# Small attentions: query, key and value projections from three products of rounded parts, and the context laid out by columns in memory

## The chip, the cores and the metric

One core of one Trainium2 chip runs the kernel. The time is device microseconds (us) of one execution. The engines are TensorE (PE; its weight loads are PEld), VectorE (DVE), ScalarE (ACT), GpSimd (POOL) and SyncE (SP), which here only issues DMAs. SBUF is the on-chip memory, PSUM the eight banks that PE writes.

## The reference

Four transformer layers, one after another, on x (32 sequences of 64 tokens, 256 wide) with a context of the same shape:

```python
x = L0(x, ctx)   # layernorm, self attention; layernorm, cross attention; layernorm, MLP (16 heads of 16)
x = L1(x, ctx)   # a recurrence over the tokens with gates, and a feed-forward part; takes states from ctx
x = L2(x, ctx, ctx)  # two cross attentions with 16 heads of 128, and an MLP
x = L3(x, ctx)   # cross attention with 16 heads of 16, and an MLP
# a small attention (L0 self, L0 cross, L3):
q = (h @ wq + bq); k = (s @ wk + bk); v = (s @ wv + bv)   # s is h or ctx; 256 x 256 weights
out = x + softmax(q @ k.T / 4, masked) @ v @ wo + bo
```

Everything is f32.

## The kernel before, in words

The 2048 tokens go in four chunks of 512 (eight sequences each). Ten stages of four chunks follow one another: self attention, cross attention, MLP, the recurrence and its feed-forward part, two large cross attentions, MLP, the third small attention, MLP. A chunk of a stage has the number `it`; a chunk of a small attention also has `ai`: 0 to 3 self, 4 to 7 cross, 8 to 11 the third. Every engine has its own program, written out by hand as generators that `run` (L364) strings together; engines meet by semaphores only, so that the order written for an engine is the order in which it works.

In a small attention one `n` is four heads of one chunk; p = n % 4 counts them within the chunk. The PE program `attention` (L460) does for each n: `scores` (L490, 32 small products of kbd and qT into banks 0 and 1), `turn` for n - 3 (L509, eight transposes of T into banks 2 and 3) and at the end `weigh` for n - 3 (L519, 32 products of vbd and PTs). Beside them stand, by p: 0, `gather` of ai - 2 and the projections 2 and 3 of ai; 1, `merge` of ai - 2 (the output projection) and `front` (the transposes of the normalised xn for the next chunk); 2, for ai below 4 `ctx_front` (the transposes of one chunk of the context), and `values` of ai + 1; 3, the projections 0 and 1 of ai + 1. Projections (`project` by `linear`, L444) and `values` (L480) are plain f32 products.

All but scores and turn take a bank from a ring of four (banks 4 to 7) in the order in which they are issued: `take` (L389) waits until the one that had the bank four takes earlier has been read by its user. In the third attention's first chunk the ring has two banks.

The other engines follow in the same order of n. DVE (L1419 on): `scale` (scores times mask into T), at p = 3 `values` (adds the bias and writes vbd, in two halves with `largest` between them), `largest` (nmax, of n - 1), `weighed` (reciprocal and a_tok, of n - 4; its end is the semaphore att_out), at p = 1 `update` (X), at p = 3 `stats`. POOL: `masked` (T plus the mask's second part), at p = 0 `roots` (ends with nmr), `lowered` (T minus the largest, of n - 1), at p = 1 `bias` (X<-X,rows). ACT: `exp` of n - 2, `turn` of n - 3 (PTs), at p = 0 `gather`, `project` and `normed` (xn), at p = 1 `front` (hT), at p = 2 the context's copy to ctxT, at p = 3 `project`.

The MLPs and the large attentions already make their products from rounded parts: a number is split into hi (rounded to the type fp32r) and lo = number - hi, and a product is hi hi + hi lo + lo hi, three products of fp32r (`SPLIT`).

## Time and profile before

| | |
|---|---|
| median of 3 runs | 2008.86 us (2006.38 to 2009.13) |
| the profiled execution | 2009.09 us |
| its span in the trace | 2007.3 us |
| PE busy | 95% |
| DVE, ACT, POOL busy | 58%, 52%, 51% |
| mean granted clock of TensorE | 0.973 |

The small attentions take the first 260 us or so and the stretch from 1770 to 1900 us. The span is what the rows below are counted in; matmuls overlap, so the duration of a row with xN is from its first start to its last end, and a mean of one is longer than the distance between two.

### The profile page before, as it was taken

The numbers are of one execution on the slowest core, as the hardware profiler recorded it, in microseconds if no ns is written. First come the engines' busy times: TensorE is split into PE (matmuls) and PEld (weight loads), VectorE is DVE, ScalarE is ACT, GpSimd is POOL, SyncE is SP. The second block draws the span as 40 slices with busy tenths as digits, with TensorE's granted clock in tenths as the row PEclk, the third lists the DMA queues.
The fourth block names the chain that finished last, engine by engine and source line by source line (L and its number), as shares of the span: only waits on it lengthen the run. The fifth ranks groups of instructions, "written<-read, shape, count | busy, mean of one in ns | idle before, by whom it ended". The sixth has DMA issues, their size and how long they took to land.

```text
span 2007.3 us, 39375 instructions
## 1 busy us (share of the span) xinstructions
PE 1901.9 (95%) x15120; PEld 1560.6 (78%) x15120; DVE 1161.2 (58%) x2104; ACT 1046.0 (52%) x1950; POOL 1013.7 (51%) x1140
## 2 busy tenths in 40 slices
PE   8999999898987699999999999999999998999999
PEld 5777789433455488898999989899998988977788
DVE  4556655489888455455545555455455546754654
ACT  4665543433342366665665655566566564445532
POOL 6776831376653255454454545445454454347630
PEclk9999999989997799999999999999999999999999
DMA  5010010000000032332323233233232320000000
GB/s 190 2 44 1 2 56 1 1 0 0 1 1 32 23 107 82 93 88 85 86 88 92 80 93 92 80 93 87 86 89 84 93 69 22 22 24 20 2 11 32
DMA packets 61847, 108.11 MB, mean 54 GB/s; under 512 B 7008, under 2 KB 42336, under 8 KB 60256
## 3 DMA queue, kind: packets, MB, share of 16 engines
q1 hardware_dynamic: 60784, 103.38, 17.0%
q8 instruction: 123, 2.02, 0.4%
q10 hardware_dynamic: 880, 2.22, 0.3%
q14 instruction: 60, 0.49, 0.1%
HBM read 103.47 MB, written 2.10 MB: 53 GB/s over the span
## 4 chain that ended last, share of the span: by engine, by line
PE 82%; DVE 9%; issue 4%; POOL 3%; ACT 2%; DMA 0%; DVEq 0%; SPq 0%; ACTq 0%; POOLq 0%
PE banks L837 19%; PE banks L866 9%; PE banks L909 9%; PE banks L611 7%; PE banks L628 6%; PE banks L447 6%; PE banks L898 6%; PE banks L879 4%; PE banks L456 3%; PE banks L529 2%; PE banks L504 2%; PE banks L486 2%; PE banks L515 2%; PE banks L433 1%; PE banks L887 1%
## 5 line engine op out<-in xcount | busy, mean ns | idle before, releaser
L1882 POOL TENSOR_TENSOR w_lo<-w2ring,w_hi 128x512 fp32r<-128x512 f32 x128 | 166.3, 1299 | 294.7 <-ACT w_hi L1098 294.7
L1322 ACT ACTIVATE PT<-banks 64x256 f32<-64x256 f32 x256 | 96.7, 378 | 262.3 <-PE banks L887 259.2
L1714 DVE SCALAR_TENSOR_TENSOR c_lo<-banks,cols,c_hi 128x512 fp32r<-128x512 f32 x128 | 96.1, 751 | 228.1 <-ACT c_hi L1288 228.1
L1962 POOL TENSOR_TENSOR wo_lo<-wo_ring,wo_hi 128x256 fp32r<-128x256 f32 x128 | 94.0, 735 | 169.1 <-ACT wo_hi L1294 169.1
L909 PE MATMUL banks<-wo_hi,c_hi 128*128 128x256 f32 x512 | 149.9, 293 | 2.7 <-POOL wo_lo L1962 2.7
L909 PE MATMUL banks<-wo_hi,c_lo 128*128 128x256 f32 x512 | 145.1, 283 | 0.0
L909 PE MATMUL banks<-wo_lo,c_hi 128*128 128x256 f32 x512 | 144.8, 283 | 0.0
L898 PEld LDWEIGHTS banks<-PT,v 128*128 128x128 f32 x1024 | 132.7, 191 | 8.9 <-ACT PT L1322 0.4
L898 PE MATMUL banks<-PT,v 128*128 128x128 f32 x1024 | 134.9, 275 | 0.3 <-ACT PT L1322 0.3
L1281 ACT ACTIVATE k<-banks,cols 128x512 f32<-128x512 f32 x128 | 87.9, 687 | 82.8 <-PE banks L837 82.7
L447 PE MATMUL banks<-xm,wl 128*128 128x512 f32 x208 | 109.2, 671 | 16.5 <-DVE xm L1643 6.3
L1723 DVE TENSOR_REDUCE nmax<-banks 128x4 f32<-128x260 f32 x128 | 54.4, 425 | 112.3 <-PE banks L879 112.2
L1920 POOL TENSOR_TENSOR rsZ<-stS,r1T 128x512 f32<-128x512 f32 x64 | 84.7, 1329 | 62.0 <-DVE stS L1591 56.9
L1707 DVE TENSOR_TENSOR v<-banks,dbv 128x512 f32<-128x512 f32 x128 | 88.5, 692 | 46.1 <-PE banks L866 41.6
L1886 POOL TENSOR_TENSOR wv_lo<-w2ring,wv_hi 128x256 fp32r<-128x256 f32 x128 | 113.6, 888 | 0.0
L866 PE MATMUL banks<-wv_hi,ctx_hi 128*128 128x256 f32 x512 | 108.2, 293 | 0.0
L1809 POOL TENSOR_TENSOR T<-T,a_pair 128x1024 f32<-128x1024 f32 x32 | 75.6, 2363 | 63.2 <-DVE T L1443 63.2
L1080 ACT ACTIVATE g_full_a<-banks,cols 128x512 f32<-128x512 f32 x64 | 44.1, 689 | 115.1 <-PE banks L628 113.2
L866 PE MATMUL banks<-wv_hi,ctx_lo 128*128 128x256 f32 x512 | 103.1, 283 | 0.0
L866 PE MATMUL banks<-wv_lo,ctx_hi 128*128 128x256 f32 x512 | 103.1, 283 | 0.0
L967 ACT ACTIVATE xn<-X,nmr,rstd 128x256 f32<-128x256 f32 x160 | 82.8, 591 | 35.5 <-POOL nmr L1777 35.5
L909 PEld LDWEIGHTS banks<-wo_hi,c_hi 128*128 128x128 f32 x512 | 98.2, 192 | 3.1 <-POOL wo_lo L1962 3.1
(224 smaller groups left out, 5599.7 us busy)
## 6 DMA issues: line engine op xcount, KB each, us to landing
w2ring<-in_w SPq DMA_DIRECT2D x128, 384.0 KB, 3.0
b2ring<-in_b SPq DMA_DIRECT2D x128, 128.0 KB, 3.5
wo_ring<-in_wo SPq DMA_DIRECT2D x128, 128.0 KB, 2.3
mlp_w<-in_mlp SPq DMA_DIRECT2D x6, 1024.0 KB, 5.0
wl<-in_wres SPq DMA_DIRECT2D x1, 2688.0 KB, 9.2
X<-in_x_in SPq DMA_DIRECT2D x4, 512.0 KB, 11.4
ctx_tok<-in_ctx_in SPq DMA_DIRECT2D x4, 512.0 KB, 16.9
wb<-in_wres SPq DMA_DIRECT2D x2, 1024.0 KB, 13.0
```

The source lines that it names most:

```text
L447: last = mm(b[0:rows_out, :], w[:, k, m0:m0 + rows_out], src[:, k, :], start=(k == 0), stop=(k == KT - 1))
L611: last = mm(bank[sums(c) + t // 2][:, t % 2 * D:(t % 2 + 1) * D], g[x][:, n % GR, t * P:(t + 1) * P], wd[y][:, i, :], start=(i == 0 and t ...
L628: last = mm(b, (w1_hi[m], w1_lo)[x][:, k, i * P:(i + 1) * P], hs[m][y][c % 2][:, k, :], start=(x, y, k) == pairs[0], stop=(x, y, k) == pai ...
L837: last = mm(b[:, :], w[i][:, k, :], src[j][:, k, :], start=(i, j, k) == pairs[0], stop=(i, j, k) == pairs[-1])
L866: last = mm(b[:, i % 2 * D:(i % 2 + 1) * D], (ctx_hi, ctx_lo)[x][:, c, k, i * P:(i + 1) * P], (wv_hi, wv_lo)[y][:, p % 2, k].rearrange("p ...
L898: last = mm(out, v2[:, n % 2, i, :], PT2[:, n % 2, i].rearrange("p r q -> p (r q)"), start=True, stop=True)
L909: last = mm(bank[6 + t // 2][:, t % 2 * D:(t % 2 + 1) * D], (c_hi, c_lo)[x][:, n % CR, t * P:(t + 1) * P], (wo_hi, wo_lo)[y][:, n % 2, :], ...
L1322: A(PT2[keys_of, n % 2, :, r, :], held(("tp2", n))[keys_of, 0:2 * P].rearrange("p (i q) -> p i q", i=NT), ACT.Copy)\
L1714: V.scalar_tensor_tensor(c_lo[:, n % CR, :], held(("pv2", n))[:, :], col(biv, n % H2), c_hi[:, n % CR, :].bitcast(f32), ALU.add, ALU.subtr ...
L1882: G.tensor_tensor(w2_lo[:, n % 2, :], w2ring[:, n % 3, 0:2 * KT * P], w2_hi[:, n % 2, :].bitcast(f32), ALU.subtract).then_inc(S["l2_wlo"], 1)
L1886: G.tensor_tensor(wv_lo[:, h, :, n % 2, :], view(w2ring[:, n % 3, 2 * KT * P:], "p (k d) -> p k d", k=KT), wv_hi[:, h, :, n % 2, :].bitcas ...
L1962: G.tensor_tensor(wo_lo[:, n % 2, :], wo_ring[:, n % WR, :], wo_hi[:, n % 2, :].bitcast(f32), ALU.subtract).then_inc(S["l2_wolo"], 1)
```

## The change

Projections and values of the three small attentions are made of three products of rounded parts. The parts are made as follows, in each engine's order:

- weights: three pieces of 128x512 per attention. ACT copies them to hi; lo is made by DVE at the start for the self attention, by POOL in the quarters p = 1, 2, 3 of self chunk 2 for the cross attention, and by POOL inside the second MLP for the third;
- the normalised input h: `normed_hi` on ACT, `normed_lo` on DVE, at p = 1 for the self chunks and at p = 2 later;
- the context, from ctxT: `attended_hi` on ACT and `attended_lo` on DVE, at p = 1 ahead of each chunk 4 to 7 and 9 to 11, and inside the second MLP for chunk 8.

h's and the context's parts have one buffer each. On PE, `front` stands ahead of `merge` at p = 1. The host lays the context out by columns, so it is loaded as ctxT; its transposes and ACT's copies of them are gone. SP loads the first half of the first MLP's weights earlier and waits for the last projections ahead of the second half.

```diff
-        ctx_tok = view(at("ctx_tok", M, CHUNKS * NT * D), "p (c t d) -> p c t d", c=CHUNKS, t=NT)
...
+        cs = [view(at(f"cs_{n}", M + 2048 + 1024 * i, KT * TOK, f32r), "p (k n) -> p k n", k=KT) for i, n in enumerate(("hi", "lo"))]
+        hs_first = [view(at(f"hs_first_{n}", A + 12544 + 1024 * i, KT * TOK, f32r), "p (k n) -> p k n", k=KT) for i, n in enumerate(("hi", "lo"))]
+        NQ = 3 * KT * D
+        aw_raw = [wa[:, 0:NQ], wb[:, 0:NQ], wb[:, 0:NQ]]
...
+        def normed_parts(ai):
+            return hs_first if ai == 2 * CHUNKS else (hs_a[0][1], hs_a[1][1])
...
-                def ctx_front(c, k):
-                    if k == 0:
-                        pe.wait_ge(s_ctx[c], 16)
-                    b = take(pe, ("ctx", c, k), "ctxT_ready", KT * c + k + 1, SINGLE)
-                    for t in range(NT):
-                        last = nc.tensor.transpose(b[:, t * P:(t + 1) * P], ctx_tok[:, c, t, k * P:(k + 1) * P], ident)
-                    last.then_inc(S["ctx_tp"], 1)
...
+                            pe.wait_ge(S["at_wlo"], 3 * (a + 1))
                         if key and ai >= CHUNKS:
-                            pe.wait_ge(S["ctxT_ready"], KT * (c + 1))
-                            return ctxT[:, c]
-                        pe.wait_ge(S["ln_hT"], KT * (it + 1))
-                        return hT2[:, it % 2]
+                            pe.wait_ge(S["at_clo"], KT * (ai - CHUNKS + 1))
+                            return cs
+                        pe.wait_ge(S["at_hlo"], KT * (ai + 1))
+                        return normed_parts(ai)
                     def project(ai, n, among):
                         m, key = QK[n]
                         w = parts[ai // CHUNKS - a0]
-                        linear(("qk", ai, n), w[1] if key else w[0], source(ai, key), m * P, "qk_mm", "qk_T", 6 * ai + QK_DONE[n], among=among)
+                        src, b = source(ai, key), take(pe, ("qk", ai, n), "qk_T", 6 * ai + QK_DONE[n], among)
+                        pairs = [(x, y, k) for x, y in SPLIT for k in range(KT)]
+                        for x, y, k in pairs:
+                            last = mm(b, w[1 if key else 0][x][:, k, m * P:(m + 1) * P], src[y][:, k, :],
+                                      start=(x, y, k) == pairs[0], stop=(x, y, k) == pairs[-1])
+                        last.then_inc(S["qk_mm"], 1)
...
+                            pairs = [(x, y, k) for x, y in SPLIT for k in range(KT)]
+                            for x, y, k in pairs:
+                                last = mm(b[:, i * D:(i + 1) * D], src[x][:, k, t * P:(t + 1) * P], wv[y][:, k, :],
+                                          start=(x, y, k) == pairs[0], stop=(x, y, k) == pairs[-1])
...
                         if p == 1:
+                            for k in range(KT):
+                                front(attended(ai) + 1, k, among)
                             if ai - 2 >= start:
                                 merge(ai - 2, among)
-                            for k in range(KT):
-                                front(attended(ai) + 1, k, among)
-                        if p == 2 and ai < CHUNKS:
-                            for k in range(KT):
-                                ctx_front(ai, k)
                         if p == 2 and ai + 1 < stop:
...
+                def weights_part_hi(a, i):
+                    if i == 0:
+                        act.wait_ge((s_w0, s_w1, s_w3)[a], 16)
+                    A(aw_hi[a][i], aw_raw[a][:, i * WP:(i + 1) * WP], ACT.Copy).then_inc(S["at_whi"], 1)
+                def normed_hi(ai):
+                    it = attended(ai)
+                    if ai not in (0, 2 * CHUNKS):
+                        act.wait_ge(S["qk_mm"], 4 * ai)
+                        act.wait_ge(S["v_mm"], 2 * min(ai, CHUNKS))
+                    if ai == 2 * CHUNKS + 1:
+                        act.wait_ge(S["acc_mm"], NT * (accumulated(CHUNKS * MLP1 + CHUNKS - 1) + 1))
+                    for k in range(KT):
+                        act.wait_ge(S["ln_hT"], KT * it + k + 1)
+                        A(normed_parts(ai)[0][:, k, :], hT2[:, it % 2, k, :], ACT.Copy).then_inc(S["at_hhi"], 1)
+                def attended_hi(ai):
+                    if ai < 2 * CHUNKS:
+                        act.wait_ge(s_ctx[ai % CHUNKS], 16)
+                    if ai == 2 * CHUNKS:
+                        act.wait_ge(S["mlp_wlo"], 2 * MT)
+                    elif ai > CHUNKS:
+                        act.wait_ge(S["qk_mm"], 4 * (ai - 1) + 3)
+                        act.wait_ge(S["v_mm"], 2 * ai)
+                    for k in range(KT):
+                        A(cs[0][:, k, :], ctxT[:, ai % CHUNKS, k, :], ACT.Copy).then_inc(S["at_chi"], 1)
...
+                            if CHUNKS <= ai + 1 < stop:
+                                attended_hi(ai + 1)
                             for k in range(KT):
                                 front(it + 1, k)
-                        if p == 2 and ai < CHUNKS:
-                            for k in range(KT):
-                                act.wait_ge(S["ctx_tp"], KT * ai + k + 1)
-                                A(ctxT[:, ai, k, :], held(("ctx", ai, k)), ACT.Copy).then_inc(S["ctxT_ready"], 1)
+                        if p == (1 if ai + 1 < CHUNKS else 2) and ai + 1 < stop:
+                            normed_hi(ai + 1)
+                        if p and ai == 2:
+                            weights_part_hi(1, p - 1)
...
+                        if m == 1 and c == CHUNKS - 1:
+                            if i == 5:
+                                for part_of in range(3):
+                                    weights_part_hi(2, part_of)
+                            if i == 6:
+                                attended_hi(2 * CHUNKS)
+                            if i == 7:
+                                normed_hi(2 * CHUNKS)
...
                 normed(0)
+                for i in range(3):
+                    weights_part_hi(0, i)
                 act.wait_ge(s_small, SMALL)
                 for k in range(KT):
                     front(0, k)
+                normed_hi(0)
...
+                def normed_lo(ai):
+                    it, (hi, lo) = attended(ai), normed_parts(ai)
+                    for k in range(KT):
+                        dve.wait_ge(S["at_hhi"], KT * ai + k + 1)
+                        V.tensor_tensor(lo[:, k, :], hT2[:, it % 2, k, :], hi[:, k, :].bitcast(f32), ALU.subtract).then_inc(S["at_hlo"], 1)
+                def attended_lo(ai):
+                    for k in range(KT):
+                        dve.wait_ge(S["at_chi"], KT * (ai - CHUNKS) + k + 1)
+                        V.tensor_tensor(cs[1][:, k, :], ctxT[:, ai % CHUNKS, k, :], cs[0][:, k, :].bitcast(f32), ALU.subtract)\
+                            .then_inc(S["at_clo"], 1)
...
                             values(ai + 1, 0)
+                        if p == 1 and CHUNKS <= ai + 1 < stop:
+                            attended_lo(ai + 1)
                         if n > UNITS * start:
                             largest(n - 1)
                         if p == 3 and ai + 1 < stop:
...
                             weighed(n - LAG - 1)
                         if p == 1 and ai - 2 >= start:
                             update(attended(ai - 2))
+                        if p == (1 if ai + 1 < CHUNKS else 2) and ai + 1 < stop:
+                            normed_lo(ai + 1)
...
                 stats(0)
+                for i in range(3):
+                    dve.wait_ge(S["at_whi"], i + 1)
+                    V.tensor_tensor(aw_lo[0][:, i * WP:(i + 1) * WP], aw_raw[0][:, i * WP:(i + 1) * WP], aw_hi[0][i].bitcast(f32),
+                                    ALU.subtract).then_inc(S["at_wlo"], 1)
+                normed_lo(0)
...
+                def weights_part_lo(a, i):
+                    pool.wait_ge(S["at_whi"], 3 * a + i + 1)
+                    cols_of = slice(i * WP, (i + 1) * WP)
+                    G.tensor_tensor(aw_lo[a][:, cols_of], aw_raw[a][:, cols_of], aw_hi[a][i].bitcast(f32), ALU.subtract)\
+                        .then_inc(S["at_wlo"], 1)
...
-                sp.wait_ge(S["ctx_tp"], KT * CHUNKS)
                 mlp_weights_up(0)
+                sp.wait_ge(S["qk_mm"], 4 * 2 * CHUNKS)
+                sp.wait_ge(S["v_mm"], 2 * 2 * CHUNKS)
                 mlp_weights_down(0)
...
-        "x_in": tokens(x), "ctx_in": tokens(enc[order]), "state": st,
+        "x_in": tokens(x), "ctx_in": enc[order].reshape(CHUNKS, TOK, KT, P).transpose(3, 0, 2, 1).reshape(P, -1), "state": st,
...
```

The order on PE at p = 1 of cross chunk 2, before: merge (wb, aT) in its two halves, then the transposes of xn.

```order
L515 MATMUL banks<-consts,T 128x128 [waits att_PT,att_exp]
L515 MATMUL banks<-consts,T 128x128 x7
L456 MATMUL banks<-wb,aT 128x256 [waits att_aT]
L456 MATMUL banks<-wb,aT 128x256 x3
L456 MATMUL banks<-wb,aT 128x256 [waits qk_T]
L456 MATMUL banks<-wb,aT 128x256 x3
L433 MATMUL banks<-consts,xn 128x128 [waits ln_xn,qk_T]
L433 MATMUL banks<-consts,xn 128x128 x3
L433 MATMUL banks<-consts,xn 128x128 [waits ln_xn,att_out]
L433 MATMUL banks<-consts,xn 128x128 x3
```

The same place after the change:

```order
L533 MATMUL banks<-consts,T 128x128 [waits att_PT,att_exp]
L533 MATMUL banks<-consts,T 128x128 x7
L452 MATMUL banks<-consts,xn 128x128 [waits ln_xn,att_aT]
L452 MATMUL banks<-consts,xn 128x128 x3
L452 MATMUL banks<-consts,xn 128x128 [waits ln_xn,qk_T]
L452 MATMUL banks<-consts,xn 128x128 x3
L467 MATMUL banks<-wb,aT 128x256 [waits qk_T,att_aT]
L467 MATMUL banks<-wb,aT 128x256 x3
L467 MATMUL banks<-wb,aT 128x256 [waits att_out]
L467 MATMUL banks<-wb,aT 128x256 x3
```

The wait att_out has moved from the second pair of transposes, last of four, to the second half of the merge, again last of four.

The order on DVE at p = 1 of a cross chunk, after the change (ACT's cs_hi and DVE's cs_lo are the context's parts; L1529 is scale, L1535 largest, L1542 and L1545 weighed, L1503 update):

```order
L1529 SCALAR_TENSOR_TENSOR T<-banks,m_pair 128x1024 [waits att_tp,att_scores]
L1478 TENSOR_TENSOR cs_lo<-ctxT,cs_hi 128x512 [waits at_chi] x2
L1535 TENSOR_REDUCE nmax<-T 128x16 [waits att_masked]
L1542 RECIPROCAL rden<-banks 128x16 [waits att_pv]
L1545 TENSOR_TENSOR a_tok<-banks,rden 128x4x64 [waits dve_step]
L1503 TENSOR_TENSOR X<-X,banks 128x512 [waits proj_mm,x_biased]
L1503 TENSOR_TENSOR X<-X,banks 128x512 [waits proj_mm]
```

Before, the row of cs_lo was not there, and the others stood in this order.

The order on ACT at p = 0 and p = 1 of a cross chunk, after the change:

```order
L1061 ACTIVATE T<-T 128x1024
L1065 ACTIVATE PTs<-banks 128x1024
L1070 ACTIVATE aT<-banks 128x512 x2
L1054 ACTIVATE kbd<-banks,cols,consts 128x512 x2
L1057 ACTIVATE qT<-banks,cols 128x512
L990 ACTIVATE xn<-X,nmr,rstd 128x256 x4
L1061 ACTIVATE T<-T 128x1024
L1065 ACTIVATE PTs<-banks 128x1024
L1034 ACTIVATE cs_hi<-ctxT 128x512 x2
L1004 ACTIVATE hT<-banks,cols 128x512 x2
```

The two copies to cs_hi are new; the others stand as before.

## Rows read from the trace of the kernel before

**Rows 1.** The page, busy us, share of the span and instructions
```profile
PE 1901.9 (95%) x15120; PEld 1560.6 (78%) x15120; DVE 1161.2 (58%) x2104; ACT 1046.0 (52%) x1950; POOL 1013.7 (51%) x1140
```

**Rows 2.** Chain of waits, cross chunk: start us, us, what
```profile
149.71 3.46 PE banks L486 x16
...
154.23 1.08 PE banks L504 x32
...
157.90 1.22 DVE nmax L1449
...
159.87 0.71 DVE vbd L1433
...
161.84 1.03 PE banks L504 x32
...
164.76 3.44 PE banks L447 x8
...
169.26 1.03 PE banks L504 x32
...
176.70 1.03 PE banks L504 x32
```

**Rows 3.** Timeline, PE in the second MLP: start us, us, instruction
```profile
1766.90 0.63 PE L628 MATMUL banks<-h_hi,w_hi_b 128*128 128x512 f32 x2
...
1768.29 0.28 PE L611 MATMUL banks<-wd_hi_b,g_hi_b 128*128 128x256 f32 x1
```

**Rows 4.** Chain of waits, second attention
```profile
732.96 2.88 PE banks L866 x24
```

**Rows 5.** Groups by form: busy us, mean ns of one, idle before
```profile
L441 PE MATMUL banks<-consts,ctx_tok 128*128 128x128 f32 x32 | 4.2, 274 | 0.0
...
L1098 ACT ACTIVATE w_hi<-w2ring 128x512 fp32r<-128x512 f32 x128 | 80.9, 632 | 4.0 <-POOL PT L1976 0.9
```

**Rows 6.** Timeline, PE in a cross chunk, quarters 3 and 1
```profile
189.75 1.13 PE L529 MATMUL banks<-vbd,PTs 128*64 128x34 f32 x32 [0.74 <-DVE vbd L1433]
...
198.23 1.10 PE L504 MATMUL banks<-kbd,qT 32*64 32x128 f32 x32
```

**Rows 7.** Timeline, the other engines there
```profile
197.23 0.20 POOL L1777 TENSOR_TENSOR nmr<-nmr,rstd 128x4 f32<-128x4 f32 x1
...
197.86 2.06 ACT L967 ACTIVATE xn<-X,nmr,rstd 128x256 f32<-128x256 f32 x4
...
200.70 2.36 POOL L1809 TENSOR_TENSOR T<-T,a_pair 128x1024 f32<-128x1024 f32 x1 [1.42 <-DVE T L1443]
200.78 1.00 ACT L1011 ACTIVATE PTs<-banks 128x1024 f32<-128x1024 f32 x1
...
201.95 0.42 DVE L1459 TENSOR_TENSOR a_tok<-banks,rden 128x256 f32<-128x256 f32 x1
```

**Rows 8.** Line 1393: ns of one, least/median/most, first and last start
```profile
L1393 DVE TENSOR_TENSOR h_lo_a<-hT,h_hi_a x16: 677/686/1219, 242.2 to 1972.7; 128x512 fp32r<-128x512 f32 x16
```

**Rows 9.** PE waits, and stretches: length, PE busy, granted clock, DMA share, GB/s
```profile
244.07 1.75 PE L529 MATMUL banks<-vbd,PTs 128*64 128x34 f32 x32 [2.94 <-ACT PTs L1011]
...
1796.40 1.95 PE L447 MATMUL banks<-ctxT,wb 128*128 128x512 f32 x4 [1.73 <-DVE vbd L1433]
...
1813.46 0.65 PE L433 MATMUL banks<-consts,xn 128*128 128x128 f32 x4 [1.64 <-DVE a_tok L1459]
...
243.00:249.00 6.00, 4.93 (x46) 0.72 0.00 0
1813.00:1823.00 10.00, 9.54 (x89) 0.66 0.01 2
1794.00:1804.00 10.00, 7.53 (x88) 1.00 0.09 16
```

**Rows 10.** Timeline, PE in the first chunk
```profile
14.88 3.67 PE L447 MATMUL banks<-hT,wa 128*128 128x512 f32 x8 [1.26 <-ACT hT L981]
...
41.85 1.13 PE L529 MATMUL banks<-vbd,PTs 128*64 128x34 f32 x32 [1.64 <-ACT PTs L1011]
```

63 lines of the change are left out of this document (47 added, 16 removed).

## The prediction

> **What bounds the kernel now.** I read the page's busy shares first: TensorE (PE) is busy 95% of the span [rows 1]. That says where to look, not what a saved PE microsecond is worth, so the chain of waits comes next, in one chunk of the cross attention [rows 2]. A chunk has four steps, which I call quarters 0 to 3 (p in the code); each does scores, turn and weigh for one group of four heads, and something beside them. The chain passes through PE in quarters 2, 0 and 1, and leaves it in quarter 3: between 154.23 and 161.84 stand VectorE's (DVE's) vbd pieces, the last at 159.87. So quarter 3 is not limited by its two projections. From these rows quarter 3 lasts 7.61 us (154.23 to 161.84), quarter 0 7.42 (to 169.26) and quarter 1 7.44 (to 176.70). Quarter 0 is scores, turn and gather, 2.92 (to 164.76), projections, 3.44, and weigh, so weigh is 1.06. Scores are 1.03 and turn and gather 0.95 each on the mean; quarter 2 is scores, turn, values and weigh, 1.03 + 1.0 + 3.46 + 1.06 = 6.55. The chunk comes to 29.0.
>
> **What the products cost.** Two f32 projections take 3.44 us (L447 x8 in [rows 2]), 1.72 each. The MLP already makes its products from three rounded pairs of the same shape; six of them take 1768.29 - 1766.90 = 1.39 us [rows 3]. So one projection saves 0.33, the two of a quarter 0.66. The values of a chunk take 3.46 in f32 (L486 x16 in [rows 2]) and 2.88 in three products (the second attention's L866 x24 [rows 4]), which saves 0.58. The turning of the context costs 4.2 us on PE for four chunks (L441 in [rows 5]), with overlap, say 0.9 per chunk. On PE alone that is 12 x (4 x 0.33 + 0.58) + 4 x 0.9 = 26 us.
> The Trainium skill, "TensorE: Matmul & The Clock Gate", section Back-to-back issue gap, gives N/2.4 + 2.5 ns for one product alone at full clock, 216 ns for 512 columns, where the rows show 232. By the page's figure 48 projections would save an estimated 4.6 us more.
>
> **Quarter 3 gives nothing.** The weigh of quarter 3 takes the bank that the second half of the values leaves, and vbd is made from it by DVE behind scale, the first half and nmax: PE already waits 0.74 for it (at 189.75 in [rows 6]). Shorter projections make that wait 1.40. Ten chunk changes lose 0.66 each: 6.6 us of the 26.
>
> **The new wait, in quarter 1.** This decides. Before a cross chunk (and before chunks 1 to 3 of the third attention) the context is split: two ScalarE (ACT) copies cs_hi, then two DVE subtractions cs_lo. Both stand in quarter 1, on DVE ahead of nmax and a_tok. The change also puts the turning of xn ahead of the merge on PE, and with that the bank that a_tok frees (the wait att_out) is asked for by the second half of the merge, no longer by the last turning.
> Count from the start of quarter 1's scores, 198.23 in [rows 6, 7]. Now: xn ends at 1.69, PTs at 3.55, a_tok at 4.14; PE needed that bank only behind the merge and four turnings, near 5.9, and never waited. After the change:
> - The quarter 0 before it is 0.66 shorter, but xn waits for POOL's nmr (ends at 197.43), which hangs on that quarter's scores and not on its projections; xn's end moves from 1.69 to about 1.96, PTs' to 3.82.
> - cs_hi: 0.63 each (w_hi, same shape [rows 5]); the first ends at 4.5.
> - cs_lo: median 0.69 each [rows 8]; POOL's mask addition (200.70, 2.36) runs until offset 4.83. They end between 5.9 and 6.3.
> - nmax 1.22 [rows 2], reciprocal and a_tok 0.67 (0.25 before 0.42), with hand-overs: a_tok ends at about 7.95.
> - PE: scores 1.03, turn 1.0, turning of xn 0.9 (eight transposes like those of the context), half a merge 1.73 (a merge has the shape of the values, 3.46): there at 4.65. It waits some 3.35 us, then half a merge and weigh (1.73 + 1.06). The quarter lasts 10.8 in place of 7.44: **+3.35**.
> Bounds: if ACT had no backlog (PTs straight behind the turn, ending at 3.25), a_tok ends at 7.3 and the cost is 2.7; if POOL holds up both subtractions for their longest, 1.22 each [rows 8], it is 4.6.
> It occurs where a merge and a split meet: at self chunk 3, cross chunks 0 to 2 and chunk 2 of the third attention, five times, +17. In chunk 1 of the third attention there is no merge, but PE already waits 1.64 there for a_tok before the second turning (at 1813.46 in [rows 9]); a_tok comes later by 7.95 - 4.14: +3.8.
>
> **The clock.** Around a PE wait of 2.94 us at 244.07 the granted clock fell: 0.72 on the mean of 243 to 249, so 0.28 x 6 = 1.7 us lost [rows 9]. Around the 1.64 us wait it was 0.66 from 1813 to 1823: 3.4 us lost. After 1.73 us at 1796.40, between dense products, it stayed at 1.00. A level of 0.5 is 1.2 GHz, and these means are mixtures of it with 2.4. A wait of 3.35 us is longer than any of these, so I take a fall at each of the five, 2.4 each, between the two: +12. In chunk 1 of the third attention it fell already. Bounds: 0, and 5 x 3.4 = 17; if quarter 3's waits of 1.4 us brought falls too, more on top.
>
> **Two engines at one memory.** The other subtractions, h_lo, come in quarter 1 of the self chunks, behind DVE's update, and in quarter 2 later. The same instruction takes 0.68 at best and 1.22 at most [rows 8]. In a self chunk they come behind the update of the merge's second half, which PE now ends later (offset 6.4 and not 5.5), and before quarter 2's scale; ACT's hT and two copies come before them. I count them as eating what the dropped turning of the context saves there, 0.9.
> The Trainium skill, "SBUF — State Buffer", section SBUF: two separate sides, says that a DVE instruction with two SBUF inputs and a POOL one that reads SBUF exclude each other for whole instructions. The range 0.68 to 1.22 agrees in kind; whether a subtraction behind a POOL instruction of 2.4 us waits for all of it, no row shows.
>
> **The sum**, against the profiled execution's 2009.09:
> - start: the first projections wait for weights and xn to be split (ACT 0.63 each, DVE 0.69 behind the last): they start near 17 instead of 14.88 [rows 10], but are 1.24 shorter with the values, and the first weigh at 41.85 hangs on PTs, not on PE: +0.3. Bounds 0 and +2.2.
> - self chunks 1 and 2: 0.66 each in quarter 0, little in quarter 2, against three POOL subtractions of weights in chunk 2: -1.
> - quarter 1: +17 and +3.8; clock: +12.
> - quarter 0 of eight later chunks: -5.3; the values in quarter 2 of seven: -4.1; the turning at self chunk 3: -0.9.
> - the third attention's start: 1.24 less on PE, but DVE has cs_lo ahead of nmax and so POOL's next step there: 0. Bounds -1.2 and +2.8.
> 0.3 - 1 + 17 + 3.8 + 12 - 5.3 - 4.1 - 0.9 = +21.8: **2031 us**. The median, 2008.86, stands within 0.3 of the execution; the sum holds for it too.
> Costed at nothing: the third attention's weights are split inside the MLP, where PE's products are the chain and ACT and DVE wait for them; its load comes three MLP steps and more ahead, and if it were late, ACT's gelu would queue behind it. SP's new wait, for the last projections, ends a chunk before the down weights are read. The first half of mlp_w is now loaded at the start, last in its queue, with nothing behind it that the first chunks need.
>
> **Rivals.** The smallest difference that a measurement can tell from none is about 0.2%, 4 us.
> 1. The wait as above, without falls of the clock: +10, 2019. For it: 1.73 us cost nothing at 1796.40. Against: 2.94 us did.
> 2. PE stays the bound. It decides if a_tok in quarter 1 ends by offset 4.65 and not at 7.95, so if cs_hi and cs_lo cost DVE no time there. Then -26 + 6.6 + 1 = -18: 1991. For it: PE's 95%, and idle time on DVE. Against: the order on DVE, and ACT's two copies behind PTs.
> 3. Falls of the clock in most other chunks too, from quarter 3's waits: eight more of 2.4, 2050. For it: 1.64 us was enough once. Against: the projections around it are dense, as at 1796.40.
> 4. DVE's two-input subtractions and POOL's instructions take turns, each waiting for the whole of the other: h_lo in quarter 2 ends some 1.1 us later and delays DVE's chain in quarter 3, seven times, and a weight of 1 us on each of five splits: +12, 2043. This is what the Trainium skill's page "SBUF — State Buffer" would make of it.
>
> **Chances.** The forecast 0.45, rival 1 0.16, rival 2 0.13, rival 3 0.09, rival 4 0.12; 0.05 that gains and losses cancel. The range of 8 in 10 reaches from 2004 (the wait at its lower bound, no fall, the small terms at their best) to 2050. Faster by over 0.2%: 0.13 (rival 2). Within 0.2%: 0.07 (cancelling, and rival 1's low end). Slower: 0.80.
>
> **What would show it.** Right: PE idle some 3 us, put down to a_tok, before the second half of the merge, five times; quarter 1 of a cross chunk near 10.8 us; cs_lo on DVE right before nmax; half clock after each; quarter 3 still 7.6. Wrong: a cross chunk of 28 us or less, or a_tok in quarter 1 within 4.7 us of the scores.

## The result, and the profile after

The changed kernel takes **2045.64 us** in the median of 4 runs (2042.92 to 2048.48), the kernel before 2008.53 beside it: a ratio of 1.0187, interval 1.0169 to 1.0205. The forecast was 2031.0 with 2004 to 2050 around it. The profiled execution's span is 2043.9 us in place of 2007.3: 36.6 us more, where the sum had 21.8.

The page of the changed kernel, busy shares and the shares of the chain of waits:

```profile
PE 1900.8 (93%) x15280; PEld 1588.6 (78%) x15280; DVE 1212.7 (59%) x2147; ACT 1068.2 (52%) x1991; POOL 1030.4 (50%) x1146
...
PE 76%; DVE 11%; issue 5%; POOL 4%; ACT 4%; DMA 0%; DVEq 0%; SPq 0%; ACTq 0%; POOLq 0%
```

PE is busy as long as before [rows 1], in fewer per cent of a longer span. That alone misleads: its products did get shorter, but products at half clock took back what that gave, and they count as busy. The waits came on top.

**Quarter 1 of a cross chunk** (timeline of the changed kernel, PE; the scores of this quarter begin at 148.44, L467 is the merge):

```profile
150.47 1.07 PE L452 MATMUL banks<-consts,xn 128*128 128x128 f32 x8
151.38 1.89 PE L467 MATMUL banks<-wa,aT 128*128 128x256 f32 x8
156.24 3.29 PE L467 MATMUL banks<-wa,aT 128*128 128x256 f32 x8 [2.97 <-DVE a_tok L1545]
```

The same stretch on DVE and POOL:

```profile
149.61 1.22 DVE L1529 SCALAR_TENSOR_TENSOR T<-banks,m_pair 128x1024 f32<-128x1024 f32 x1 [3.93 <-PE banks L522]
152.74 1.70 DVE L1478 TENSOR_TENSOR cs_lo<-ctxT,cs_hi 128x512 fp32r<-128x512 f32 x2 [1.90 <-ACT cs_hi L1034]
154.36 1.20 DVE L1535 TENSOR_REDUCE nmax<-T 128x16 f32<-128x1024 f32 x1
...
155.76 0.42 DVE L1545 TENSOR_TENSOR a_tok<-banks,rden 128x256 f32<-128x256 f32 x1
...
150.92 2.37 POOL L1915 TENSOR_TENSOR T<-T,a_pair 128x1024 f32<-128x1024 f32 x1 [0.84 <-DVE T L1529]
```

DVE idles 1.90 us for cs_hi, then does cs_lo, and only then nmax and a_tok, which ends 7.7 us behind the scores where it ended at 4.14 [rows 7]. PE stands before the second half of the merge for 2.97 us; that half then takes 3.29 us where it took 1.89 in front of the wait. The clock (stretches of the changed kernel: length, PE busy, PEld, DVE, ACT, POOL, granted clock, DMA share, GB/s):

```profile
17.00:24.00 7.00, 6.52 (x20) 5.39 (x21) 2.03 (x9) 2.47 (x4) 2.69 (x5) 0.52 1.03 403
58.00:68.00 10.00, 9.80 (x92) 9.10 (x93) 6.39 (x7) 6.26 (x9) 8.23 (x4) 0.50 0.01 2
153.00:163.00 10.00, 7.03 (x84) 5.47 (x83) 5.53 (x8) 2.62 (x5) 4.49 (x3) 0.83 0.01 2
187.00:203.00 16.00, 13.35 (x132) 11.95 (x134) 9.89 (x13) 4.96 (x7) 8.92 (x4) 0.68 0.00 1
1874.00:1886.00 12.00, 9.04 (x138) 7.45 (x134) 5.91 (x8) 7.36 (x11) 8.44 (x4) 1.00 0.00 1
```

The first two stretches are the start and self chunk 1, which come up again below. The last three lie around three of the five waits of 2.96 to 2.98 us. Granted 0.5 is the level of 1.2 GHz. At one the fall cost 1.6 us, at one 4.6 (the products stayed at half clock up to 201), at the last nothing.

**Places that the forecast did not price.** Self chunk 0, timeline of the changed kernel, PE, DVE and POOL:

```profile
37.84 0.79 PE L504 MATMUL banks<-aw_hi,h_hi_a 128*128 128x256 f32 x2 [4.09 <-DVE h_lo_a L1473]
...
33.83 3.96 DVE L1473 TENSOR_TENSOR h_lo_a<-hT,h_hi_a 128x512 fp32r<-128x512 f32 x2 [0.20 <-ACT h_hi_a L1022]
...
32.58 2.35 POOL L1915 TENSOR_TENSOR T<-T,a_self 128x1024 f32<-128x1024 f32 x1 [1.16 <-DVE T L1529]
34.88 2.36 POOL L1920 TENSOR_TENSOR T<-T,nmax 128x1024 f32<-128x1024 f32 x1
37.20 2.82 POOL L1883 TENSOR_TENSOR X<-X,rows 128x1024 f32<-128x1024 f32 x1
```

and the third attention's first chunk (PE waited 1.73 us here before the change, at 1796.40 in [rows 9]):

```profile
1827.04 1.19 PE L493 MATMUL banks<-cs_hi,aw_hi 128*128 128x512 f32 x2 [6.53 <-DVE vbd L1519]
...
1819.29 5.15 DVE L1473 TENSOR_TENSOR h_lo_a<-hT,h_hi_a 128x512 fp32r<-128x512 f32 x2 [2.08 <-ACT h_hi_a L1022]
1824.37 1.21 DVE L1529 SCALAR_TENSOR_TENSOR T<-banks,m_pair 128x1024 f32<-128x1024 f32 x1
...
1816.90 2.38 POOL L1883 TENSOR_TENSOR X<-X,rows 128x1024 f32<-128x1024 f32 x1
1819.23 2.36 POOL L1915 TENSOR_TENSOR T<-T,a_pair 128x1024 f32<-128x1024 f32 x1
1821.54 2.36 POOL L1920 TENSOR_TENSOR T<-T,nmax 128x1024 f32<-128x1024 f32 x1
```

Two subtractions of 0.68 us each take 3.96 us together in one place and 5.15 in the other, and each of them ends 0.55 us behind the end of a POOL instruction. All 28 of the changed kernel's h_lo and cs_lo subtractions that took over 0.72 us end like this, 0.55 or 0.56 us behind one. It is not only that they start late: once started they stand behind POOL.

Where the 36.6 us lie, by the starts of the scores on PE (a chunk runs from its first scores to the next chunk's; "last" is to its last scores; us). The other columns are the experiments' profiled runs; that of late_one was the slowest of its four, 2000.0 us where their median is 1994.9:

| stretch | before | after | cs_late | merge_first | one_input | late_one | ctx_alone | early_f32 |
|---|---|---|---|---|---|---|---|---|
| first scores | 21.9 | 26.1 | 24.9 | 26.2 | 24.6 | 25.7 | 23.2 | 22.1 |
| self chunks 0 to 2 | 80.9 | 82.1 | 83.3 | 82.8 | 74.8 | 76.7 | 79.5 | 77.4 |
| self 3, cross 0 to 2 | 117.0 | 135.9 | 114.6 | 122.4 | 123.4 | 112.2 | 116.2 | 111.9 |
| cross 3, last | 19.2 | 18.7 | 18.7 | 18.7 | 18.8 | 18.7 | 19.2 | 19.2 |
| to third, chunk 1 | 1563.0 | 1570.9 | 1572.0 | 1569.8 | 1565.9 | 1566.4 | 1563.0 | 1564.0 |
| third, chunk 1 | 30.5 | 33.6 | 29.4 | 33.7 | 33.0 | 26.3 | 27.3 | 26.7 |
| third, chunk 2 | 29.0 | 31.8 | 28.7 | 30.6 | 30.9 | 28.0 | 29.0 | 28.0 |
| third, chunk 3, last | 19.2 | 18.7 | 18.7 | 18.6 | 18.7 | 18.8 | 19.2 | 19.2 |
| last scores to the end | 126.6 | 126.1 | 126.5 | 126.9 | 126.5 | 125.4 | 126.5 | 126.6 |

### The profile page after: what moved, and what is told of

Read it like the earlier page. It is cut to its first block, busy times and chain, and to the rows that moved or that the text cites. A ratio compares the mean times of both kernels' runs of the same rounds, so it can differ in the third digit from the quotient of the medians.

```text
span 2043.9 us, 39820 instructions
## 1 busy us (share of the span) xinstructions
PE 1900.8 (93%) x15280; PEld 1588.6 (78%) x15280; DVE 1212.7 (59%) x2147; ACT 1068.2 (52%) x1991; POOL 1030.4 (50%) x1146
## 4 chain that ended last, share of the span: by engine, by line
PE 76%; DVE 11%; issue 5%; POOL 4%; ACT 4%; DMA 0%; DVEq 0%; SPq 0%; ACTq 0%; POOLq 0%
PE banks L852 18%; PE banks L881 9%; PE banks L924 9%; PE banks L626 6%; PE banks L643 6%; PE banks L913 6%; PE banks L894 4%; PE banks L458 3%; PE banks L467 3%; PE banks L547 1%; PE banks L504 1%; PE banks L902 1%; PE banks L452 1%; POOL T L1915 1%; PE banks L522 1%
## 5 line engine op out<-in xcount | busy, mean ns | idle before, releaser
L1348 ACT ACTIVATE k<-banks,cols 128x512 f32<-128x512 f32 x128 | 88.0, 688 | 82.8 <-PE banks L852 82.6
L1818 DVE TENSOR_REDUCE nmax<-banks 128x4 f32<-128x260 f32 x128 | 54.4, 425 | 112.2 <-PE banks L894 112.0
L1915 POOL TENSOR_TENSOR T<-T,a_pair 128x1024 f32<-128x1024 f32 x32 | 76.7, 2398 | 69.6 <-DVE T L1529 69.6
L1920 POOL TENSOR_TENSOR T<-T,nmax 128x1024 f32<-128x1024 f32 x48 | 95.3, 1988 | 17.7 <-DVE nmax L1535 17.5
L458 PEld LDWEIGHTS banks<-xm,wl 128*128 128x128 f32 x208 | 42.7, 215 | 75.6 <-issue 55.9
## 6 DMA issues: line engine op xcount, KB each, us to landing
wb<-in_wres SPq DMA_DIRECT2D x2, 1024.0 KB, 12.6
```

Source lines behind the costliest of these rows:

```text
L458: last = mm(b[0:rows_out, :], w[:, k, m0:m0 + rows_out], src[:, k, :], start=(k == 0), stop=(k == KT - 1))
L1915: G.tensor_tensor(t, t, m, ALU.add).then_inc(S["att_masked"], 1)
```

## The experiments

Two causes were to be told apart: the order on DVE (and on PE) that makes a_tok late, and the turns that DVE and POOL take. A third question came up later: whether quarter 3 can be made to give what PE saves. Times are medians; each ratio is against the kernel before on the same chip.

### cs_late: the order on DVE

```diff
-                        if p == 1 and CHUNKS <= ai + 1 < stop:
-                            attended_lo(ai + 1)
                         if n > UNITS * start:
                             largest(n - 1)
...
                             weighed(n - LAG - 1)
+                        if p == 1 and CHUNKS <= ai + 1 < stop:
+                            attended_lo(ai + 1)
```

> The changed kernel with one thing moved on DVE: in quarter 1 the two cs_lo come behind a_tok (and ahead of X), no longer ahead of nmax. Theory A (DVE's order makes the wait): a_tok falls back to some 4.2 us behind the scores, PE finds its bank free when it comes at 4.65, and the quarters 1 that took 12.2 to 12.4 us take about 7.5; five of them, some 24 us with their falls of the clock, and 3.5 us in chunk 1 of the third attention, less what the values then wait for cs_lo in quarter 2 (0 to 1 us each): near 2020. Theory B (PE's order makes it: front ahead of merge is what hurts, whatever DVE does): the wait stays, within 3 us of 2045.6.

Measured: **2017.68 us**, ratio 1.0049 (1.0032 to 1.0066), 28 us less than the change. Theory A. The same place in its timeline, DVE and then PE:

```profile
145.99 1.21 DVE L1535 TENSOR_REDUCE nmax<-T 128x16 f32<-128x1024 f32 x1
147.12 0.25 DVE L1542 RECIPROCAL rden<-banks 128x16 f32<-128x16 f32 x1
147.40 0.42 DVE L1545 TENSOR_TENSOR a_tok<-banks,rden 128x256 f32<-128x256 f32 x1
147.97 3.41 DVE L1478 TENSOR_TENSOR cs_lo<-ctxT,cs_hi 128x512 fp32r<-128x512 f32 x2
...
146.61 3.62 PE L467 MATMUL banks<-wa,aT 128*128 128x256 f32 x16
```

a_tok ends 4.1 us behind the scores (143.68), the merge is one piece, quarter 1 is 7.54 us in all five places, and the clock does not fall there. cs_lo itself now takes 3.41 us, twice what it took, and in the cross chunks nobody waits for it; at the third attention's start, where POOL has a backlog, PE waits 3.17 us for it.

### merge_first: the order on PE

```diff
+                            if ai - 2 >= start:
+                                merge(ai - 2, among)
                             for k in range(KT):
                                 front(attended(ai) + 1, k, among)
-                            if ai - 2 >= start:
-                                merge(ai - 2, among)
```

> The changed kernel with PE's order at quarter 1 put back: merge ahead of the turning of xn. Theory A (DVE's order makes a_tok late): a_tok still ends some 7.6 us behind the scores; PE asks for its bank at about 6.4 instead of 4.65, so 1.2 us of waiting are left of 2.97 in each of five quarters, 9 us less, and if the clock then stays up another 8 or so: 2028 to 2037. Theory B (PE's order makes it): the wait is gone and quarter 1 is 7.5, near 2020.

Measured: **2033.52 us**, ratio 1.0133 (1.0110 to 1.0156). Theory A again. The wait is 1.78 us where 1.2 was expected, and quarter 1 is 9.55. One of five alike (timeline, PE), and the stretch around it (the granted clock is the number behind POOL's):

```profile
154.26 0.66 PE L452 MATMUL banks<-consts,xn 128*128 128x128 f32 x4 [1.78 <-DVE a_tok L1545]
```

```profile
154.00:158.00 4.00, 3.56 (x75) 3.14 (x76) 2.17 (x4) 1.72 (x2) 3.88 (x2) 1.00 0.03 6
```

a_tok still ends 7.7 us behind the scores (154.21 against 146.47). So its lateness is DVE's; the swap on PE made the wait 1.2 us longer, and the falls of the clock came with the longer wait only.

### one_input: DVE and POOL take turns

```diff
-                        V.tensor_tensor(lo[:, k, :], hT2[:, it % 2, k, :], hi[:, k, :].bitcast(f32), ALU.subtract)...
+                        V.tensor_reduce(lo[:, k, :].unsqueeze(2), hT2[:, it % 2, k, :].unsqueeze(2), AX, ALU.max)...
```

and the same for cs_lo. The low part then holds the number itself: the kernel leaves out the subtraction.

> The changed kernel, but h_lo and cs_lo are made by a DVE instruction of the same shape that reads one SBUF tensor and not two (the low part holds a copy of the number: hi is not subtracted). Nothing is moved. Theory C (a DVE instruction with two SBUF inputs and a POOL instruction take turns for whole instructions): the pairs of h_lo that take 3.5 to 5.2 us take 1.3 to 1.5, the waits of 4.09 us at 37.8 and 6.53 us at 1827 shrink to 1.5 and 2, cs_lo loses 0.5; in all 10 to 18 us less, 2028 to 2036. Theory D (those instructions are slow because they come late, behind ACT's h_hi, or for their shape): durations and time stay, 2045 within 2.

Measured: **2018.90 us**, ratio 1.0064 (1.0042 to 1.0087), 27 us less than the change, more than either theory had. One line of the trace each, first of the changed kernel, then of this one (ns of one: least/median/most):

```profile
L1473 DVE TENSOR_TENSOR h_lo_a<-hT,h_hi_a x22: 677/2027/2848, 15.9 to 1890.4; 128x512 fp32r<-128x512 f32 x22
```

```profile
L1473 DVE TENSOR_REDUCE h_lo_a<-hT x22: 675/677/687, 16.0 to 1862.3; 128x512 fp32r<-128x512 f32 x22
L1478 DVE TENSOR_REDUCE cs_lo<-ctxT x16: 670/676/686, 110.6 to 1852.2; 128x512 fp32r<-128x512 f32 x16
```

At the same places in the program and at the same least duration, the form with one SBUF input never takes more than 0.69 us; the one with two has a median of 2.03. Theory C. The operation was changed with the inputs, but the form of the operation is not the reason: in the changed kernel subtractions and sums of the same kind (TENSOR_TENSOR) with one input in PSUM keep their time beside POOL or not: X<-X,banks takes 0.69 us at most in all 72 places and vbd 0.70 in all 48. The Trainium skill's page "SBUF — State Buffer", section SBUF: two separate sides, says that such a DVE instruction and a GpSimd one hold a port pair in turn for the whole instruction; this trace agrees, with 2848 against 687 ns. POOL pays too: its subtraction of the largest takes 1.90 us, but 2.35 to 2.38 in the eight places where one of DVE's subtractions ends just inside it (34.88 above is one).

Of the 27 us, 7.3 lie in self chunks 0 to 2, 12.5 in the four chunks from self 3 on, and 5 on the way to the third attention's chunk 1 (table). The 1.5 at the start are not the edit's: PE's first wait is 3.09 us where it was 3.19, and cs_late, whose start is the changed kernel's, has its first scores at 24.9 too, because the clock stayed down for less long. The 12.5 are more than the subtractions lost: in quarter 1 they gave back 0.4 us, the wait fell from 2.97 to 2.55, and the clock stayed up (timeline of this kernel, PE, and the stretch around it):

```profile
144.52 1.99 PE L467 MATMUL banks<-wa,aT 128*128 128x256 f32 x8 [2.55 <-DVE a_tok L1545]
```

```profile
144.00:148.00 4.00, 3.48 (x58) 2.95 (x62) 1.81 (x4) 1.06 (x1) 4.00 (x2) 1.00 0.03 6
```

### late_one: both together

> cs_late and one_input together: cs_lo behind a_tok on DVE, and h_lo and cs_lo as instructions that read one SBUF tensor (hi is not subtracted). cs_late alone took 28 us off, one_input alone 27. If each removes the same wait in quarter 1 (its five falls of the clock and its length), they overlap: of one_input's 27 some 10 lie in quarter 1 and are already gone, some 15 lie in the self chunks, quarter 3 and the third attention's start and are left: 2001 to 2005. If the two were separate costs: near 1991. If DVE's order was all of it: no less than 2015.

Measured: **1994.92 us**, ratio 0.9931 (0.9914 to 0.9947). Off the change 51 us, where the two alone took 28 and 27: nearly additive in the medians, and 6 to 10 us below the 2001 to 2005 of the expectation's first case. The overlap is there where it was expected: in the four chunks from self 3 on the two take off 21.3 and 12.5 alone and 23.7 together. With cs_lo out of quarter 1, the rest of what POOL holds up is in the self chunks (83.3 to 76.7) and around the third attention's start (1572.0 to 1566.4, and 29.4 to 26.3). Part of the last is luck: the wait of 1.54 us in chunk 1 brought no fall of the clock here, the one of 1.57 in cs_late did. The trace, from an execution 5 us above the median, can't place the rest. This is what three products would be worth if a low part cost DVE 0.68 us and never a turn behind POOL. It doesn't compute the low part, so it is a bound and not a version.

### ctx_alone: the other half of the change

Projections and values are f32 products of hT and ctxT again, no parts are made, and merge stands ahead of front as in the kernel before. P3 lists the attentions that make three products; here it is empty:

```diff
+        P3 = []
...
+                        if ai // CHUNKS not in P3:
+                            for k in range(KT):
+                                last = mm(b, w[1 if key else 0][:, k, m * P:(m + 1) * P], src[:, k, :], start=(k == 0), stop=(k == KT - 1))
+                            last.then_inc(S["qk_mm"], 1)
+                            return
```

> Only the context by columns is kept (no turning on PE, no copies on ACT); all projections and values are f32 products of the unsplit inputs, and merge stands ahead of front as in the kernel before. If PE bounds the self chunks' quarter 2, 0.9 us less in each of four: 2005. If the self chunks' waits for other engines take it up: within 1 us of 2008.5. A loss would be against both: then the loads, not the products, cost something.

Measured: **2006.37 us**, ratio 0.9992 (0.9982 to 1.0001): no difference that can be told, on the side of the gain. In the trace quarter 2 of self chunks 1 to 3 is 6.57 us in place of 7.44, but the first scores are 1.3 us later in this run. The 3.2 us less in the third attention's chunk 1 are not the edit's: the same wait of 1.64 us as in [rows 9] brought no fall of the clock this time. So none of the 36.6 us can be put down to the context's layout.

### vbd_all and vbd_f32: can quarter 3 give something?

On top of cs_late (vbd_all), and on top of ctx_alone (vbd_f32):

```diff
                             values(ai + 1, 0)
+                            values(ai + 1, 1)
...
-                        if p == 3 and ai + 1 < stop:
-                            values(ai + 1, 1)
```

> cs_late with one thing more on DVE: in quarter 3 both halves of vbd come ahead of nmax (before, nmax stood between them). Theory E (quarter 3 gives nothing because the weigh at its end waits for the second vbd, and only for that): its two waits on vbd, 0.95 and 1.06 us, go, the quarter falls from 8.2 to 6.0 to 6.3, ten times, so 19 to 22 us less than cs_late: near 1997, and a cross chunk is 26.3 to 26.7 us. Theory F (DVE as a whole bounds the chunk; what it does not do in quarter 3 it does later): the chunk stays above 28 us and the time above 2010.

> The same order on DVE (both halves of vbd ahead of nmax) with f32 products throughout, the context by columns and merge ahead of front. The wait of 0.74 us on vbd in quarter 3 goes and nothing else: 7.60 to 6.87, ten times, so 6 to 8 us less than the context alone: near 1999. The difference between this and vbd_all then says what the three products are worth when nothing waits; by PE's own durations 12 x (4 x 0.33 + 0.58) = 23 us, less what self chunks and the third attention's start lose.

Measured: vbd_all **2016.56 us** (1.0044, 1.0029 to 1.0059), vbd_f32 **2005.55** (0.9988, 0.9979 to 0.9998). Theory E falls as it stood. Quarter 3 did shrink, from 8.2 to 7.06 and from 7.60 to 6.80, but quarter 0 grew, from 6.9 to 8.0 and from 7.42 to 8.02, and the chunk stayed at 28.6 and 28.8. PE in quarters 3 and 0 of vbd_all:

```profile
161.93 0.70 PE L493 MATMUL banks<-h_hi_a,aw_hi 128*128 128x512 f32 x2 [0.95 <-DVE vbd L1519]
...
169.96 0.70 PE L493 MATMUL banks<-h_hi_a,aw_hi 128*128 128x512 f32 x2 [1.04 <-DVE a_tok L1545]
```

The second wait for vbd turned into one for a_tok, which stands behind nmax and behind the statistics of quarter 3. In vbd_f32 the wait for vbd is gone and one of 0.36 us for a_tok has come. The figures of theory F came true for vbd_all (a chunk above 28 us, more than 2010), but they don't show its reason: DVE is busy for 24.3 of a cross chunk's 28.65 us in cs_late, and what PE waits for is one place in DVE's order.

### vbd_cross and vbd_two: three products in some attentions only

The order of vbd_all; three products in the cross attention alone, and in the cross and the third.

> As vbd_all, with three products in the cross attention alone; the self attention and the third make f32 products of unsplit inputs. Theory C (the loss at the start and in the self chunks comes from h_lo, which POOL holds up): the first scores come back to some 22 to 23 us, the self chunks save the 5.3 us that they cost more in cs_late than before, cross chunks are 26.3 to 26.7 us, the third attention as in vbd_f32: 1988 to 1993. If the splitting of the cross weights in self chunk 2 costs something of its own, self chunk 2 is longer than in vbd_f32 by that.

> As vbd_cross, with three products in the third attention too. Its chunks 1 to 3 gain about 1.9 us each, but its first chunk loses 5 to 6 us (in cs_late it took 30.8 us where the kernel before took 25.2) and the second MLP some 2 us for the splitting of its weights: 1 to 3 us above vbd_cross. If the loss of the first chunk comes from vbd standing behind nmax, this order mends it, and the kernel is 3 to 5 us below vbd_cross.

Measured: **2004.73 us** (0.9983, 0.9974 to 0.9993) and **2009.49** (1.0006, 0.9997 to 1.0015). Leaving the self attention out brings back the start (first scores at 23.1 and 23.6, not 25.8 as in vbd_all); leaving the third out is worth 4.8 us, more than the 1 to 3 expected; vbd_two's other branch (a gain) did not happen, and the third attention's first chunk still waits for cs_lo. Chunks of the cross attention are 28.6 us and not 26.3 to 26.7, for the reason seen in vbd_all: that part of the expectation fell with theory E.

### early_f32, early_two and best: no bank held by DVE's order

```diff
+                        if p == 3 and ai + 1 < stop:
+                            values(ai + 1, 0)
+                            values(ai + 1, 1)
                         scale(n)
+                        if n - LAG - 1 >= UNITS * start:
+                            weighed(n - LAG - 1)
                         if n > UNITS * start:
                             largest(n - 1)
...
-                        if p == 3 and ai + 1 < stop:
-                            stats(it + 2)
+                        if p == 0 and ai > start:
+                            stats(it + 1)
```

early_f32 makes f32 products throughout, with merge ahead of front, and has POOL's roots behind its subtraction of the largest. (best leaves the statistics and POOL's order alone.)

> f32 products throughout, the context by columns, merge ahead of front, and DVE's order rearranged: in quarter 3 both halves of vbd ahead of scale, a_tok ahead of nmax in each quarter, the statistics in quarter 0 instead of 3; on POOL the roots behind the subtraction of the largest. Theory G (quarters 3 and 0 are bound by DVE's order, which holds two of PE's banks, and the waits of vbd_f32 moved from quarter 3 to 0 with the a_tok that stands behind nmax): quarter 3 falls to 6.8 and quarter 0 stays 7.4, a chunk is 28.3 and not 29.0, ten chunks: 7 us below ctx_alone, near 1999. Theory F (DVE as a whole is the bound): no change, 2006.

Measured: **1997.46 us**, ratio 0.9944 (0.9929 to 0.9959): theory G, and the fastest kernel of the study that leaves nothing out, and faster than both versions of the case. Its chain of waits through a cross chunk is PE alone:

```profile
123.06 3.44 PE banks L508 x8
126.49 1.06 PE banks L572 x32
127.55 1.03 PE banks L547 x32
128.58 1.02 PE banks L558 x8
129.60 0.87 PE banks L583 x8
130.48 3.44 PE banks L508 x8
```

A chunk is 27.98 us in place of 29.04. Theory F (DVE as a whole) is ruled out for f32 products: DVE works 17.5 us in such a chunk before and after. Not all of the gain is this: the third attention's chunk 1 has lost its wait of 1.64 us and the fall of the clock that followed it (30.5 to 26.7 in the table).

> The same order, with three products in the cross attention and the third (the self attention keeps f32 products). Theory G: with no bank held, a cross chunk takes PE's own 6.9 + 7.5 + 6.0 + 5.9 = 26.3 us instead of the 28.65 of cs_late and the 29.04 of the kernel before: against early_f32 some 2 us less in each of seven chunks, 14, and 5 to 7 us more for the third attention's start: near 1991. Theory F: a chunk above 28.3 and a time of 2005 or more.

Measured: **2032.17 us**, ratio 1.0116 (1.0101 to 1.0131). Theory F's figures (2005 or more, a chunk above 28.3) are met and theory G's are not, but the reason is again one place in DVE's order. Quarters 3 and 0 are as G said, 5.86 and 6.74; quarter 1 took 12.6:

```profile
185.10 1.93 PE L572 MATMUL banks<-vbd,PTs 128*64 128x34 f32 x32 [4.30 <-DVE X L1545]
...
180.82 3.54 DVE L1520 TENSOR_TENSOR cs_lo<-ctxT,cs_hi 128x512 fp32r<-128x512 f32 x2 [2.33 <-ACT cs_hi L1072]
184.28 1.27 DVE L1545 TENSOR_TENSOR X<-X,banks 128x512 f32<-128x512 f32 x2
```

With merge ahead of front the weigh takes the bank that X frees, and X stands behind cs_lo. The same mechanism as in the change, at another bank.

> Three products in the cross attention alone, front ahead of merge as in the changed kernel, and on DVE: in quarter 3 both halves of vbd ahead of scale, in every quarter a_tok ahead of nmax, and cs_lo behind both; statistics and roots stay where they were. In early_two the weigh of quarter 1 waited 4.3 us because merge ahead of front gave it the bank that X frees, and X stands behind cs_lo on DVE. Theory G (only orders on DVE held PE's banks): here that bank is hT's, nothing waits, and the cross chunks take early_two's other quarters, 6.7 to 6.9, 7.5, 6.0 and 5.9 to 6.5: 26.3 to 26.9 us against 28.0 in early_f32, so 5 to 7 us below its 1997.5, 1990 to 1993, below both kernels. Theory F (DVE's total work bounds a chunk with splits): cross chunks above 28 us, 1997 or more.

Measured: **1999.98 us**, ratio 0.9964 (0.9950 to 0.9978). Theory G fails for this kernel with splits and F's figures (above 28 us, 1997 or more) are met: nothing waits for X any more, but the cross chunks are 29.9 us. PE waits 0.81 for a_tok, 1.17 for xn and 1.04 to 1.10 for vbd in each. On DVE the splits take this long:

```profile
169.41 4.66 DVE L1520 TENSOR_TENSOR cs_lo<-ctxT,cs_hi 128x512 fp32r<-128x512 f32 x2 [1.42 <-ACT cs_hi L1072]
...
178.06 3.67 DVE L1513 TENSOR_TENSOR h_lo_a<-hT,h_hi_a 128x512 fp32r<-128x512 f32 x2
```

The two pairs are 8.3 us of DVE in a chunk where their own work is 2.7, and DVE is taken for 25.4 of the 29.9 us. That these waits would go with the 5.6 us is argued from the trace; best was not run with one-input low parts. The gain of best over the kernel before comes from the f32 attentions, which have the new order on DVE: by its trace 5 us less in self chunks 0 to 2 and 6.6 in the third attention (in part a fall of the clock that did not come), against 1.6 more from self chunk 3 to the end of the cross attention.

## Why the prediction was right and where it fell short

The direction, the mechanism and its place held; the sum was 14.8 us short. By its steps:

- **What the products cost.** Right for the values (quarter 2 is 5.98 us in place of 6.57, 0.59 for 0.58), too good for the projections: quarter 0 is 6.91 in place of 7.42 where nothing else came in, 0.51 for 0.66. Six products take 1.54 us here (144.29 to 145.83 on the changed kernel's PE) and 1.39 in the MLP's rows. Over eight chunks that is 1.2.
- **The new wait in quarter 1**, +3.35 each, five times. Right: where the clock stayed up (third attention, chunk 2) quarter 1 took 10.78 us, 3.34 more than before. a_tok was put at 7.95 and came at 7.7. cs_late shows that DVE's order makes it; merge_first, that 1.2 us of it need PE's order as well.
- **The clock**, +12. Measured against that 10.78: 1.5, 1.6, 4.6, 1.4 and 0, together 9.2. A mean of 2.4 was near, "a fall at each of the five" wasn't.
- **Quarter 3 gives nothing**, 7.6 us. It gave less: 8.1 us in four of the chunks and 7.6 elsewhere, because h_lo in quarter 2 is held up by POOL and scale starts late; in one_input it is 7.6 everywhere. That is rival 4's mechanism, and 2 us.
- **The start**, +0.3 with bounds 0 and +2.2. Wrong: +4.2. PE waited 3.19 us for h_lo (1.26 for hT before [rows 10]) and came out of it at half clock up to about 23.6. The start of the projections was forecast well (near 17, measured 17.48); the term left out the clock. A wait of 3.1 to 3.6 us brought the fall in all six kernels that split h at the start, and the first scores lie between 24.6 and 26.2 in them, by how long it lasted.
- **Self chunks 1 and 2**, -1. Wrong: +1, and chunk 0, not in the sum, +0.2. **"I count them as eating what the dropped turning saves"** is the step that failed: h_lo was priced at 0.68 to 1.22 us [rows 8], from rows in the MLP, where POOL seldom works beside it, and took 3.5 to 4.0 us a pair here. PE waited 4.09 us for it in chunk 0 and 1.63 in chunk 2, and in chunk 1, where it came late anyway, 2.00 for xn, with the clock at 0.50 from 58 to 68. one_input gives 7.3 us back in self chunks 0 to 2, late_one 6.6 against cs_late.
- **The third attention's start**, 0. Wrong: +5.4 from its first projections (1795.97, before 1769.72) to its second chunk. cs_lo and h_lo stand among POOL's longest uninterrupted row of instructions and push vbd back; 6.53 us of waiting, where 1.73 was. Chunk 1, put at +2.6 with its gains, came to +3.2.
- **Work costed at nothing.** 23.8 us of the difference were there when the cross attention ended, 25.4 at 727 us (702 before), and 26.25 when the third attention's projections began. The 1.6 in between arose in code that the change does not touch (mean granted clock 0.90 there, 0.92 before). From the end of the cross attention to the same place the other kernels' traces, f32 ones among them, differ by up to 3.1 us; why, no run here settles. The other 0.85 is the change's: behind the second MLP PE waits for the context's low part,

```profile
1795.97 0.70 PE L493 MATMUL banks<-cs_hi,aw_hi 128*128 128x512 f32 x2 [0.69 <-DVE cs_lo L1478]
```

and every kernel that makes three products in the third attention has this wait (0.67 to 0.72 us), none of the others. The forecast had priced the splitting there at nothing.

These differences account for the distance. To the 21.8 of the sum come -2.8 for the clock at the five waits, +3.9 at the start, +2.2 in self chunks 0 to 2, +2.0 in quarter 3, +1.2 in quarter 0, +5.4 and +0.6 in the third attention, +0.85 and +1.6 on the way to it: 36.8, where 36.6 was measured.

Rival 1 (no falls) had the right wait and was contradicted by the clock. Rival 2 (PE stays the bound, 1991) comes near late_one's 1994.9: its size was about right for a kernel whose low parts stand behind a_tok and cost DVE no turn. Rival 4 (2043) was nearest in time. Its mechanism is real, but it doesn't replace the forecast's: the two add, and its cost lies more in the self chunks and the third attention's start than in quarter 3, where the rival had put it.

Not tried, and so open: a low part made without a second SBUF input (from the bank in PSUM, or by another engine), which is what late_one's bound would ask for.

## What to carry to other kernels

Before PE's products are made cheaper, write down which bank each waits for and what stands ahead of the instruction that frees it on its own engine; a pair of subtractions put there cost more than all the products saved, and moving them three instructions later gave 28 us. Price an elementwise DVE instruction with two SBUF operands by what POOL does at that moment, not by its duration elsewhere in the trace. And where a shortened stretch doesn't shorten the chunk (quarter 3), the next wait is the thing to look at: the order vbd, scale, a_tok, nmax on DVE, with the statistics moved to quarter 0 and f32 products, took the kernel below both versions.

## What the runs showed of the hardware

- DVE with two SBUF inputs beside POOL: 677 to 2848 ns for one 128x512 subtraction; a reduction with one SBUF input, 675 to 687. Each subtraction that waited ended 0.55 us behind the end of the POOL instruction, in the changed kernel and, counting 36 of 36, in cs_late. Instructions with one SBUF input or with one beside PSUM kept their time: in the kernel before, scale took 1.23 us at 1793.71 and nmax 1.22 at 1796.28, while POOL worked from 1791.94 to 1800.3 without a break.
- A copy with one SBUF input is not free of it: the MLP's rounding copies on DVE take 0.43 us in the median, and six that began 0.8 us into POOL's X (2.40 us) took 1.87 or 1.88. One of them, POOL and DVE:

```profile
1781.64 2.40 POOL L1883 TENSOR_TENSOR X<-X,rows 128x1024 f32<-128x1024 f32 x1 [2.23 <-ACT xn L990]
...
1782.45 1.88 DVE L1601 CAST g_hi_b<-g_full_b 128x512 fp32r<-128x512 f32 x1 [0.47 <-ACT g_full_b L1139]
```

- Waits of 2.96 to 2.98 us in the same surroundings brought a fall of the clock four times in five, with a cost of 1.4 to 4.6 us; waits of 2.55 us (one_input) and 1.78 us (merge_first) brought none in five places each, and one of 1.64 us in the third attention's chunk 1 did in the kernel before and in vbd_f32 and did not in ctx_alone. A single wait doesn't tell what it will cost.
